# First layer of a two-layer block: VectorE's tile steps interleaved with the row mixing, the last tile mixed on TensorE

## What is computed

```python
xn = layernorm(x)                      # rows of x
corr = irfft(|rfft(xn)|^2)             # autocorrelation of each row
w, delay = top_k(corr, 6)
s = sum_j softmax(w)[j] * roll(xn, -delay[j])          # "row mixing"
h = relu(xn @ up_w)**2
z = h @ down_w + (xn @ fc1_w @ expert_w) * (sum of top-2 of xn @ gate_w) @ fc2_w
x1 = x + s * silu(layernorm(z) * gamma + beta)
```

## Time and profile before

| | |
|---|---|
| runs | 2089.02, 2088.9, 2087.4 us; median 2088.9 |
| profiled execution | 2086.14 us, its span 2084.3 us |
| busy, share of the span | PE 95%, PEld 76%, DVE 77%, ACT 71%, POOL 59% |
| mean granted TensorE clock | 0.978 of full speed |
| chain of work that ended last | PE 74% of the span |
| layer 0 | from 0 to about 221 us of the span |

### The profile page before, as it was taken

One profiled execution on the slowest core, in us unless ns is written; L12 is line 12 of the kernel. 1 busy time (PEld: TensorE's weight loads), 2 busy tenths in 40 slices (PEclk: granted clock), 3 DMA queues, 4 the chain that ended last, 5 costly groups with the idle time before them and its releaser, 6 DMA issues.

```text
span 2084.3 us, 32775 instructions
## 1 busy us (share of the span) xinstructions
PE 1970.3 (95%) x10874; PEld 1587.2 (76%) x10874; DVE 1602.6 (77%) x3002; ACT 1471.8 (71%) x2946; POOL 1226.0 (59%) x848
## 2 busy tenths in 40 slices
PE   6988698989899999999999999999999999999986
PEld 4563465767688888888888888888888888888875
DVE  8557787875678787878778777888787878778776
ACT  4242675644777787878778787878787878778774
POOL 5525464753465666566566656665666565566655
PEclk9999799999999999999999999999999999999998
DMA  5504323243333334333343423333333333343433
GB/s 179 194 29 131 108 78 109 92 141 125 98 131 118 102 115 129 113 112 116 103 127 102 136 93 127 112 129 115 103 118 125 112 114 118 99 127 107 134 108 115
DMA packets 114328, 242.00 MB, mean 116 GB/s; under 512 B 23665, under 2 KB 24689, under 8 KB 113522
## 3 DMA queue, kind: packets, MB, share of 16 engines
q1 hardware_dynamic: 110322, 227.32, 33.6%
q0 software_dynamic: 3840, 12.59, 2.0%
HBM read 227.01 MB, written 12.85 MB: 115 GB/s over the span
## 4 chain that ended last, share of the span: by engine, by line
PE 74%; DVE 2%; issue 1%; ACT 1%; DVEq 0%; ACTq 0%
PE s_ps L71 13%; PE s_ps L73 13%; PE s_ps L72 13%; PE s_ps L1708 6%; PE s_ps_o L73 6%; PE s_ps_o L71 6%; PE s_ps_o L72 6%; PE s_ps L1678 5%; PE s_ps L1716 4%; PE s_ps L1670 3%; PE s_ps L1698 1%; PE s_ps L1656 1%; PE s_ps L1662 0%; ACT s_lm L1788 0%; DVE s_hdt L1922 0%
## 5 line engine op out<-in xcount | busy, mean ns | idle before, releaser
L2090 POOL TENSOR_TENSOR w_lo<-w_raw,w_hi 128x1024 fp32r<-128x1024 f32 x142 | 340.0, 2400 | 550.5 <-ACT w_hi L1770 550.5
L71 PE MATMUL s_ps<-h_hi,w_hi 128*128 128x512 f32 x1152 | 464.8, 403 | 9.2 <-DVE s_hid L1939 6.1
L73 PE MATMUL s_ps<-h_hi,w_lo 128*128 128x512 f32 x1152 | 452.2, 393 | 0.0
L72 PE MATMUL s_ps<-h_lo,w_hi 128*128 128x512 f32 x1152 | 450.5, 391 | 0.0
L1934 DVE SCALAR_TENSOR_TENSOR s_cv<-s_ps,s_par,s_cv 128x511 f32<-128x511 f32 (+2 forms) x480 | 355.9, 744 | 19.0 <-ACT s_cv L1813 13.2
L2107 POOL TENSOR_TENSOR s_lm<-s_lm,s_cbt 128x512 f32<-128x512 f32 x256 | 326.8, 1300 | 12.5 <-ACT s_lm L1795 12.5
L1788 ACT ACTIVATE s_lm<-s_rows,s_steps 128x128 f32<-128x128 f32 x1024 | 312.4, 390 | 2.2 <-PE s_ps L1708 2.2
L1813 ACT ACTIVATE s_cv<-s_ps,s_par 128x512 f32<-128x512 f32 x160 | 124.5, 778 | 227.7 <-PE s_ps L73 227.7
L71 PEld LDWEIGHTS s_ps<-h_hi,w_hi 128*128 128x128 f32 x1152 | 217.6, 189 | 55.7 <-DVE s_hid L1939 6.9
L73 PEld LDWEIGHTS s_ps<-h_hi,w_lo 128*128 128x128 f32 x1152 | 217.4, 189 | 47.8
L72 PEld LDWEIGHTS s_ps<-h_lo,w_hi 128*128 128x128 f32 x1152 | 218.0, 189 | 41.6
(11 more groups left out here) (266 smaller groups left out, 4119.0 us busy)
## 6 DMA issues: line engine op xcount, KB each, us to landing
w_raw<-in_w_in SPq DMA_DIRECT2D x144, 512.0 KB, 3.6
s_rows<-acs_dram SPq DMA_DIRECT2D x256, 256.0 KB, 4.4
s_wo_raw<-in_w_out SPq DMA_DIRECT2D x128, 256.0 KB, 3.3
w_raw<-in_gu_q SPq DMA_DIRECT2D x14, 512.0 KB, 3.5
f_d_q<-in_d_q SPq DMA_DIRECT2D x28, 256.0 KB, 2.6
f_d_w<-in_d_s SPq DMA_DIRECT2D x28, 256.0 KB, 3.4
table<-shifted SPq DMA_DIRECT2D x16, 256.0 KB, 3.0
xs<-in_x SPq DMA_DIRECT2D x8, 256.0 KB, 6.1
```

The source lines that it names most:

```text
L71: nc.tensor.matmul(dst, l_hi, r_hi, start=start, stop=False)
L72: nc.tensor.matmul(dst, l_hi, r_lo, start=False, stop=False)
L73: return nc.tensor.matmul(dst, l_lo, r_hi, start=False, stop=stop)
L2090: nc.gpsimd.tensor_tensor(w_lo[:, slot, :], w_raw[:, slot, :], w_hi[:, slot, :].bitcast(F32), ALU.subtract).then_inc(w_lo_ready, 1)
```

## The change

Six edits, all within `layer0`:

1. Late and early `uv` rows: the second half of tiles 0 to 3 is scaled by ScalarE instead of VectorE, and both halves of tiles 4 to 7 (with `shift` = -2 mean rstd, one small VectorE instruction more). ScalarE does the early ones ahead of `dft_hi` and the late ones behind `act_root(1)`, ahead of its first relu.
2. On VectorE `tokens(0)` now stands ahead of `dve_up_pairs(1)`, and the late `dve_uv` are gone. On ScalarE `act_power(0)` moves from ahead of the first relu to behind the late tiles' high parts.
3. The squares of batch 1's spectrum go into the upper half of `hid` instead of `power`, and no longer wait for `x1_ready`; its fifth relu waits for `power_ready` instead.
4. The tile steps of VectorE become functions (`added`, `affine`, `gated`) and are laced with the mixing in both batches; ScalarE's steps follow.
5. Tile 7 is no longer mixed on VectorE: `mix(1, 3)` ends after the weights. ScalarE writes six diagonal matrices (identity times weight, 128x128) into `hid`, and TensorE sums diagonal times shifted rows over six matmuls into a `ps_d` bank (`d_mix`).
6. Semaphore counts follow.

```diff
+        def squares(n): return hid[:, TB:, :] if n else power
@@ tensor
+            g = NT - 1
+            turn(dve_took, d_mix)
+            pe.wait_ge(act_row_ready, NT + TB + 1)
+            pe.wait_ge(gathered[g % 2], 16 * TOPK * (g // 2 + 1))
+            for j in range(TOPK):
+                mm = nc.tensor.matmul(ps_d[:, d_mix % 4, :], hid[:, j, 0:P], shifted[:, g % 2, j, :],
+                                      start=(j == 0), stop=(j == TOPK - 1))
+            mm.then_inc(pe_d, 1)
@@ scalar
             act_root(0)
+            act.wait_ge(var_ready, TB + 1)
+            for t in range(TB):
+                act.wait_ge(sd_ready, t + 1)
+                nc.scalar.activation(uv[:, t, D // 2:], uv[:, t, D // 2:], ACT.Copy,
+                                     scale=rstd[:, t:t + 1]).then_inc(act_row_ready, 1)
             act.wait_ge(dft_loaded, 16)
...
-                    if n:
-                        act.wait_ge(x1_ready, (n - 1) * TB + m + 1)
-                    nc.scalar.activation(power[:, m, :], ps_a[:, i % 4, :], ACT.Square).then_inc(act_took, 1)
+                    nc.scalar.activation(squares(n)[:, m, :], ps_a[:, i % 4, :], ACT.Square).then_inc(act_took, 1)
...
                     act_root(1)
-                act_power(n)
+                    act.wait_ge(var_ready, VARS)
+                    for t in range(TB, NT):
+                        act.wait_ge(sd_ready, t + 1)
+                        nc.scalar.activation(uv[:, t, 0:D // 2], uv[:, t, 0:D // 2], ACT.Identity,
+                                             bias=shift[:, t:t + 1], scale=rstd[:, t:t + 1])
+                        nc.scalar.activation(uv[:, t, D // 2:], uv[:, t, D // 2:], ACT.Copy,
+                                             scale=rstd[:, t:t + 1]).then_inc(act_row_ready, 1)
+                else:
+                    act_power(n)
...
+                    if n and m == TB:
+                        act.wait_ge(power_ready, 5 * (n + 1))
...
                         for t in range(TB, NT):
                             act.wait_ge(pe_d, d_turn(t) + 1)
-                            act_turned(t, ps_d[:, d_turn(t) % 4, :], late_hi_ready)
+                            act_turned(t, ps_d[:, d_turn(t) % 4, :], act_row_ready)
+                        act_power(n)
...
+                act_routed(n, 0)
+                act_std(n, 0)
+                for t in range(1, TB):
+                    act_routed(n, t)
+                    act_silu(n, t - 1)
+                    act_std(n, t)
+                    if n == NB - 1 and t == 2:
+                        g = NT - 1
+                        act.wait_ge(pe_d, d_shared(n, 0) + 1)
+                        act.wait_ge(mixed_ready, g + 1)
+                        for j in range(TOPK):
+                            ins = nc.scalar.activation(hid[:, j, 0:P], ident[:], ACT.Copy, scale=top[:, g, j:j + 1])
+                        ins.then_inc(act_row_ready, 1)
+                act_silu(n, TB - 1)
@@ vector
             dve_rstd(1)
-            for t in range(TB, NT):
-                dve_uv(t)
-            dve_up_pairs(1)
+            nc.vector.scalar_tensor_tensor(shift[:, TB:], mean2[:, TB:], -1.0, rstd[:, TB:], ALU.mult,
+                                           ALU.mult).then_inc(var_ready, 1)
...
             tokens(0)
+            dve_up_pairs(1)
             dve_up_lo(1)
...
                 mix(n, 0)
+                added(n, 0)
                 mix(n, 1)
+                affine(n, 0)
+                added(n, 1)
+                mix(n, 2)
+                if n == NB - 1:
+                    mix(n, 3)
+                gated(n, 0)
+                affine(n, 1)
+                added(n, 2)
+                if n < NB - 1:
+                    mix(n, 3)
+                gated(n, 1)
+                affine(n, 2)
+                added(n, 3)
+                gated(n, 2)
+                affine(n, 3)
+                gated(n, 3)
```

More of the change, by code:

```diff
@@ L123, in layer0 @@
         mean2 = sb("mean2", [P, NT])
+        shift = mean2
         std = sb("std", [P, NT])
@@ L576, in mix, with added, affine, gated @@
                 add.then_inc(mixed_ready, 1)
+            def added(n, t):
+                g, i = n * TB + t, d_shared(n, t)
+                dve.wait_ge(pe_d, i + 1)
+                dve.wait_ge(act_took, a_rout(n, t) + 1)
+                nc.vector.tensor_tensor(z[:, t, :], ps_d[:, i % 4, :], routed[:, t % 2, :], ALU.add).then_inc(z_ready, 1)
+                dve.wait_ge(z_ready, g + 1)
+                nc.vector.bn_stats(stats[:, 0, :], z[:, t, :]).then_inc(dve_took, 1)
+                dve.wait_ge(dve_took, i + 1)
+                link(nc.vector.bn_aggr(mv[:, g, :], stats[:, 0, :]))
+                nc.vector.tensor_scalar(mv[:, g, 1:2], mv[:, g, 1:2], EPS, None, ALU.add).then_inc(var_ready, 1)
+            def affine(n, t):
+                g = n * TB + t
+                dve.wait_ge(std_ready, 2 + g + 1)
+                link(nc.vector.reciprocal(rstd[:, g:g + 1], std[:, g:g + 1]))
+                link(nc.vector.scalar_tensor_tensor(z[:, t, :], z[:, t, :], mv[:, g, 0:1], gamma[:],
+                                                    ALU.subtract, ALU.mult))
+                nc.vector.scalar_tensor_tensor(z[:, t, :], z[:, t, :], rstd[:, g:g + 1], beta[:],
+                                               ALU.mult, ALU.add).then_inc(affine_ready, 1)
+            def gated(n, t):
+                g = n * TB + t
+                dve.wait_ge(silu_ready, g + 1)
+                if g == NT - 1:
+                    dve.wait_ge(pe_d, d_mix + 1)
+                else:
+                    dve.wait_ge(mixed_ready, g + 1)
+                rows = ps_d[:, d_mix % 4, :] if g == NT - 1 else mixed[:, t, :]
+                link(nc.vector.tensor_tensor(mixed[:, t, :], rows, z[:, t, :], ALU.mult))
+                nc.vector.tensor_tensor(x1[:, g, :], x1[:, g, :], mixed[:, t, :], ALU.add).then_inc(x1_ready, 1)
+                dve.wait_ge(x1_ready, g + 1)
+                link(nc.vector.bn_stats(stats[:, 1, :], x1[:, g, :]))
+                link(nc.vector.bn_aggr(x1_mv[:, g, :], stats[:, 1, :]))
             dve.wait_ge(rows_loaded, 80)
```

101 lines of the change are left out of this document (33 added, 68 removed).

## The result

The changed kernel takes 2066.3 us (median of 4 runs, 2064.5 to 2067.8), the kernel before on the same chip 2088.15 (4 runs, 2086.2 to 2089.0): ratio 0.9896, 95% interval 0.9879 to 0.9913. The forecast was 2070, its range began at 2067.

A forecast was written before the change was run, and what follows sets the result against it. Layer 0 was taken as bound by TensorE waiting for VectorE, then by VectorE at the tail, with layer 1 fixed. Terms 8.1 + 0.9 + 9.6 = 18.6 gave 2067.5 in the profile, 2070 as median; range 2067 to 2074, with (a) 2077.

The forecast's parts named there:

- Term 1: Layer 0's head and late tiles: earlier start, no stall, no slow clock behind it; shared products 8.1 us earlier.
- the four `upw_lo` (6.88) stay slow: VectorE's weight splitting in the head: still 6.88 us, 1.7 each, as GpSimd works beside it in both orders.
- 8 x 1.3 = 10.4 ... cost nothing, slack 2.6: VectorE's eight `xn` scalings beside GpSimd: 10.4 us, ending at 57.7, rows stored by about 62, before the gather at 64.6.
- rival (a): `xn` scalings each wait for nearly two GpSimd instructions, take 19.5, end at 67, delaying the gather: 2076; chance 0.09.
- Term 2: Batch 0's mixing: steps laced into VectorE's waits for gathered rows win 3.3 us, less 2.4 for `gated(0, 2)`: 0.9.
- Term 3: Tail of batch 1: last tile's mixing off VectorE and waits filled with another tile's work, 9.6 us.
- The rule that counts a drain at each table change: ScalarE's silu and root switches: about 2.66 us each, last silu 0.5 late, sum 18.1; the prediction used 1.28.
- The sum for layer 0: Layer 0's whole gain: 8.1 + 0.9 + 9.6 = 18.6 us.
- what layer 0 gives up moves the end one for one: Layer 1, untouched and busy on TensorE without a gap, was taken to pass on layer 0's gain in full.
- read against the median by adding 2.8: From profile to median: the runs' median lay 2.8 us above the profiled execution, so 2067.5 became 2070.3.
- Rival (c): Layer 1 loses clock as TensorE starts after 8 us of rest, not 24; at 2% lower, 2101; chance 0.03.
- (d): The barrier into layer 1 or its first loads absorb the gain: 2087 to 2091; chance 0.04.

The follow-up runs named there:

- e17: The kernel before, unaltered, run again with its own profile on another chip; 2086.5 us.
- e18: The changed kernel itself again, unaltered, beside e17 on the same chip; 2067.05 us against 2085.2 for the kernel before.
- e10: The change with the late rows (tiles 4 to 7) scaled by VectorE again, behind `tokens(0)`; 2075.8 us on a chip that held ScalarE back.
- e14: The change with batch 1's squares in the old buffer behind `x1_ready` again, without the fifth relu's new wait; 2073.8 us, the change there 2072.6.
- e4: The change with ScalarE's squares of batch 1 ahead of batch 0's third-tile silu and its gate-product read behind the fourth root; 2056.2 us.
- e3: The change with tile 7 mixed wholly on VectorE again, without ScalarE's diagonals and TensorE's six matmuls; 2075.3 us.
- e8: The change with batch 1's tile steps in the old unlaced order on VectorE and ScalarE; 2072.8 us, the change 2065.5.
- e1: The change with 24 more row statistics at VectorE's end of layer 0; 2084.4 us, the kernel before 2086.6.
- e6: The change with 8 more row statistics at VectorE's end of layer 0; 2071.6 us, the change there 2065.5.
- e13: The changed kernel itself again, unaltered, on a chip that held ScalarE back; 2072.6 us.

## Why the prediction was right and wrong

**Term 1, 8.1 forecast, 9.25 measured.** Right in its steps: the spectrum at 15.08 (15.2), ScalarE's 0.4 a scaling, the stall and the slow transposes gone, the upper up products at once behind them. Mis-sized: "the four `upw_lo` (6.88) stay slow" took 5.77, and that is the 1.0 by which up was earlier than said. The 6.88 is no fixed price of the kernel before: in e17, the same kernel, it took 5.77, and in e18, the change again, 5.22. Wrong in its cause: the stall was put down to the scaling as much as to the order, and e10 shows that the order alone ends it. Moving `act_power(0)` also takes GpSimd's work from beside VectorE's scalings.

**The step "8 x 1.3 = 10.4 ... cost nothing, slack 2.6" failed.** The eight `xn` took 14.05, and the table was late: without it the gather would have gone at about 63.5 (its first top-k is at 60.72, and before, with the table in time, the gather went 2.76 us behind the first top-k), with it at 66.20. Two prices were wrong. A mean of 1.3 for each scaling was taken from rows beside single GpSimd instructions, and here one scaling of 7.50 us stood beside a whole run of them. This is rival (a)'s mechanism, and worse than its two instructions for each scaling, but it struck one scaling hard and spared the last four, so they ended at 59.5 and not at 67. And from the end of the scalings to the gather it is 6.7 us (59.54 to 66.20), where the prediction had 4.3 until the rows are stored and nothing for the 2.6 us behind the last store. The cost is 2.0 to 2.7 us, less than half of what (a) had said, and it ate the surplus of term 1.

**Term 2** is 0.8 from the gather on (53.41 to 52.62), as said, and -1.9 with the late table in it. That the new place of the squares is worth nothing is right (e14); that their wait stays "at about 6" is low: it is 8.8, and the term did not ask what it would be worth to remove: e4 did.

**Term 3, 9.6 forecast, 10.4 measured**, 9.5 from the rows of tile 5 on, and 0.9 before them. Its parts hold one by one: 4.46 for the last tile (4.4; e3), 5.3 for the lacing (5.2; e8), TensorE's mixing 5.39 (5.4). The rule that counts a drain at each table change (the Trainium skill, ScalarE: Activation LUTs, What ACT_TABLE_LOAD costs) would have made the last silu 0.5 later, as an estimate; VectorE waited 0.70 for it, as before, and the last root stands at 196.05, directly behind its load of 1.28 at 194.76, so the trace goes with 1.28.

**The sum for layer 0, 18.6, came out as 17.68.** What put the time below the range are the two steps that carry it from layer 0 to the median. The first is "what layer 0 gives up moves the end one for one". A delay does move the end one for one (e1, e6), but layer 1 is no constant. Its length went from 1859.8 to 1866.0 between kernels that don't differ in it, with the granted clock of a stretch of 280 us, and "stretches ... without a pause" at 1.00 said nothing on the first 360 us. In the first comparison layer 1 was 3.3 us shorter. The second is "read against the median by adding 2.8": that was the distance of one profile from its median, and it was 1.1 behind the change (2065.16 and 2066.3), 1.7 less. So 2070.3 + 0.9 - 3.3 - 1.7 = 2066.2. Either of the two alone would have left the time inside the range (2067.9 or 2069.5). In two other comparisons the whole gain was 18.9 and 18.2, about what the sum had said, but that is partly luck: in the second of them layer 0 gave 16.0 and the part behind it 3.2. What sets the length of layer 1 stays open. Rival (c) looked at the right place with the wrong sign and cause: a pause of 25.6 us or of 2.6 made no difference beyond the scatter. (d) is refuted: e6 gave 6.1 for 5.8 us of delay.

## What to carry to other kernels

When a step moves, ask what it will stand beside, on both engines: the same eight scalings cost 2.3 us beside an idle GpSimd and 6.1 beside a busy one, and the `xn` tiles went from 4.90 to 14.05 without being touched. A mean over such instructions misleads: look at the longest single one, and at whether the other engine's work comes in pieces or in one run. When an edit frees a value from a wait, look at once at what else stands ahead of it in its engine's queue; here the buffer alone was worth nothing, and with the order changed as well it was worth 10 us. And before a gain is read to the last 3 us, know how much the untouched part of the program scatters, by kernel and by chip, and how far a single profile lies from the median of the runs.

## What was not expected of the hardware

Identical instructions behind layer 0 took 1859.8 to 1866.0 us at mean clocks of 0.97 to 0.95 over 280 us. On two of five chips ScalarE stood up to 12.5 us behind a finished product, which cost the change 6 to 7 us. One 128x512 scaling on VectorE took 7.50 us beside an unbroken run of GpSimd's, 0.53 with GpSimd idle. TensorE's twelve matmuls took 5.39 us behind a pause of 0.70 at a granted clock of 1.00, 7.08 behind one of 4.11 (e13) and 7.39 behind one of 9.01 at 0.73 (e8).
